# Loading stacked attention operands in fewer, taller pieces, storing their parts earlier, and reordering the router, the output projection and the last layers

## What is computed

```python
x = x + _layernorm(_L0_attn_ref(_layernorm(x), wq, wk, wv, wo))        # 16 heads of 64, causal softmax
x = x + _layernorm(_L0_ffn_ref(_layernorm(x), router_w, ...))          # 8 experts of 256, top 2, capacity 640
x = x + _layernorm(_L1_attn_ref(_layernorm(x), qkv, wo))               # 16 heads of 8, rotary, causal softmax
x = x + _layernorm(_L1_ffn_ref(_layernorm(x), fast_b, w_fc, w_proj, u, v, gate))
# _L1_attn_ref, last line:  out.transpose(0, 2, 1, 3).reshape(B, S, D) @ wo.T
# _L1_ffn_ref:  h = bitlinear(x, w_fc) + gate * (x @ v.T @ fast_b.T @ u.T);  r = max(h, 0);  bitlinear(r * r, w_proj)
```

## Time and profile before

| | us |
|---|---|
| three runs | 1238.11, 1240.81, 1241.08; median 1240.81 |
| the profiled execution | 1239.13 |
| its span from first to last instruction | 1237.3 |
| PE busy | 1121.1 (91%) |
| DVE busy | 862.2 (70%) |
| ACT busy | 815.4 (66%) |
| POOL busy | 349.4 (28%) |
| first attention | up to about 545 |
| output projection, norms, router, second biases | 545 to 613 |
| experts | 613 to 738 |
| second attention | 748 to 1174 |
| output projection, norms, last feed-forward | 1174 to 1237 |

### The profile page before, as it was taken

How to read it: one execution, slowest core, us unless ns; L and a number is a source line. 1 busy time by engine, 2 the same in 40 slices (tenths; PEclk the granted TensorE clock), 3 DMA queues, 4 the chain that set the end, 5 groups by cost and what they waited for, 6 DMA issues and landing times.

```text
span 1237.3 us, 28186 instructions
## 1 busy us (share of the span) xinstructions
PE 1121.1 (91%) x10202; PEld 851.2 (69%) x10202; DVE 862.2 (70%) x2486; ACT 815.4 (66%) x1915; POOL 349.4 (28%) x345
## 2 busy tenths in 40 slices
PE   5999999999999999999899976987888888888886
PEld 3787878787888787888576653665566556556674
DVE  6656566565656565645334547999999899999863
ACT  3766666767666666631233434998889889989932
POOL 1974646455464646213001202000000000000043
PEclk8999999999999999999599995998999899999998
DMA  6222223222322323211011043020310202110001
GB/s 161 59 69 76 69 58 77 63 59 64 80 54 70 76 59 75 65 36 34 15 35 43 25 97 46 2 40 27 66 31 10 40 6 36 26 15 2 2 1 34
DMA packets 33627, 58.90 MB, mean 48 GB/s; under 512 B 4906, under 2 KB 18114, under 8 KB 33490
## 3 DMA queue, kind: packets, MB, share of 16 engines
q1 hardware_dynamic: 32690, 55.52, 19.9%
q10 hardware_dynamic: 800, 1.57, 0.4%
HBM read 27.59 MB, written 4.33 MB: 26 GB/s over the span
## 4 chain that ended last, share of the span: by engine, by line
PE 56%; DVE 18%; issue 11%; ACT 7%; POOL 5%; DMA 2%; SPq 1%; ACTq 0%; POOLq 0%; DVEq 0%
PE pT L1278 12%; PE pO L1201 12%; PE pS L1239 10%; DVE Zb L956 9%; PE pS L1352 4%; ACT probs L719 3%; PE pT L1149 3%; PE pT L1365 3%; DVE Sm L971 3%; PE pS L1313 2%; PE pT L1153 2%; PE pS L1430 1%; ACT PT L699 1%; PE pS L1410 1%; DMA KS<-split 1%
## 5 line engine op out<-in xcount | busy, mean ns | idle before, releaser
L1278 PE MATMUL pT<-cst,probs 128*128 128x128 f32 x2304 | 369.9, 287 | 53.4 <-ACT probs L719 49.2
L1278 PEld LDWEIGHTS pT<-cst,probs 128*128 128x128 f32 x2304 | 257.0, 143 | 149.0 <-ACT probs L719 99.7
L719 ACT ACTIVATE probs<-probs,nmax 128x128 f32<-128x128 f32 (+7 forms) x256 | 198.7, 776 | 129.9 <-DVE nmax L966 128.9
L699 ACT COPY PT<-pT 128x512 f32<-128x512 f32 (+3 forms) x576 | 263.9, 482 | 16.8 <-PE pT L1278 15.6
L966 DVE CUSTOM_DVE_ANT_0 probs<-pS,causal_wide 128x128 f32<-128x128 f32 (+7 forms) x256 | 192.0, 750 | 91.2 <-PE pS L1239 83.6
L719 ACT ACTIVATE probs<-Sm,nmax 128x128 f32<-128x128 f32 (+7 forms) x256 | 199.6, 780 | 55.4 <-DVE nmax L971 49.1
L1201 PE MATMUL pO<-PT,V 128*64 128x128 f32 (+1 forms) x4608 | 233.5, 281 | 2.5 <-DVE attnT L925 1.1
L956 DVE TENSOR_SCALAR Zb<-pS 128x128 bf16<-128x128 f32 (+7 forms) x256 | 192.7, 753 | 20.0 <-PE pS L1245 19.4
L1201 PEld LDWEIGHTS pO<-PT,V 128*64 128x64 f32 (+1 forms) x4608 | 180.9, 114 | 36.3 <-issue 21.0
L971 DVE CUSTOM_DVE_ANT_0 Sm<-pS,Zb 128x128 f32<-128x128 f32 (+7 forms) x256 | 193.3, 755 | 4.5
L543 POOL TENSOR_TENSOR rstd<-rstd,power 128x4 f32<-128x4 f32 x32 | 32.6, 1019 | 552.4 <-DVE rstd L824 552.4
(11 more groups left out here) (189 smaller groups left out, 1370.2 us busy)
## 6 DMA issues: line engine op xcount, KB each, us to landing
wq_t<-factors SPq DMA_DIRECT2D x32, 256.0 KB, 4.0
Qs<-Ql SPq DMA_DIRECT2D x30, 256.0 KB, 3.7
Kh<-Kh SPq DMA_DIRECT2D x30, 256.0 KB, 3.4
Kl<-Kl SPq DMA_DIRECT2D x30, 256.0 KB, 4.6
QS<-split SPq DMA_DIRECT2D x72, 64.0 KB
KS<-split SPq DMA_DIRECT2D x72, 64.0 KB
w1s<-in_w SPq DMA_DIRECT2D x16, 128.0 KB, 2.3
w2s<-in_w SPq DMA_DIRECT2D x16, 128.0 KB, 2.2
```

The source lines that it names most:

```text
L699: nc.scalar.copy(PT[:, g % 2, h, k0 * P:(k0 + nk) * P], pT[r % TBANKS][:, 0:nk * P])\
L719: nc.scalar.activation(probs[:, i % NPROB, 0:n], src[:, 0:n], ACT.Exp, bias=nmax[:, i % 4:i % 4 + 1], scale=-1.0, accum_out=total).then_in ...
L1278: m = nc.tensor.transpose(pT[r % TBANKS][:, kt * P:(kt + 1) * P], probs[:, item % NPROB, (k0 + kt) * P:(k0 + kt + 1) * P], ident)
```

## The change

- **Stacks.** The DRAM tensor is laid out by heads, and the query parts are written three times, once for each key part they are paired with (`split_q`), so that the 72 rows of QS lie behind one another. `stacks` issues 2 loads for QS (64 and 8 rows) and 3 for KS (24 rows each). The bytes loaded are the same.
- **Stores.** One part at a time: 3 DMAs for a query part and 1 for a key part, 12 for a batch (3.1 MB, before 1.6 MB). Those of the first batch move from ACT's queue to SP's, around the loads of the last expert's weights: part 0 of both ahead of w1 of m = 15, the others between w1 and w2.
- **Output projection of the second attention.** SP gathers the 16 heads' rows of `attn1T` into a tile `compact` (4 copies of 8 rows by 4 KB for each half, 32 in all, issued behind the loads of the stacks), and one product for each tile replaces four.
- **Router.** The preparation of `w1e`, `w2e` and `lowA` moves behind `up(0)` on PE and behind `gelus(0)` on ACT; the logits of bank j - 1 are computed right after the transposes of bank j. A wait for the copies of `w1e` and `w2e` stands before the third bank of the gate weights' transposes.
- **Last feed-forward.** The first products of bank j come ahead of the second product of bank j - 1. The normed input goes to `xn3`, another place.

```diff
-        split = nc.dram_tensor("split", (2, PARTS, D, T), BF16, kind="Internal").ap()
+        split_q = nc.dram_tensor("split_q", (HEADS, PARTS, PARTS, DH1, T), BF16, kind="Internal").ap()
+        split_k = nc.dram_tensor("split_k", (HEADS, PARTS, DH1, T), BF16, kind="Internal").ap()
...
+            def store(i, parts):
+                cols = slice(i // 2 * S, (i // 2 + 1) * S)
+                for k in parts:
+                    if k < 2:
+                        sp.wait_ge(part_a, split_step_of(i, k))
+                    else:
+                        sp.wait_ge(part_v, split_step_of(i, 1))
+                    for to in [split_q[:, k, j, :, cols] for j in range(PARTS)] if i % 2 == 0 else [split_k[:, k, :, cols]]:
+                        sp.dma_start(to, part_of(i)[:, k, :]).then_inc(part_stored, 16)
+
             for m in range(2, B * E):
                 e = m % E
+                if m == B * E - 1:
+                    store(0, (0,))
+                    store(1, (0,))
                 sp.wait_ge(up_done, (m - 1) * per_batch)
                 sp.dma_start(w1s[:, m % 2, :], w1[e, :, :]).then_inc(ld_w1[m % 2], 16)
+                if m == B * E - 1:
+                    store(0, (1, 2))
+                    store(1, (1, 2))
                 sp.wait_ge(down_done, (m - 1) * (S // BANK))
...
+                q_rows = split_q[heads, :, :, :, cols].rearrange("h i j d s -> (i j d) h s")
+                k_rows = split_k[heads, :, :, cols].rearrange("h j d s -> (j d) h s")
+                for lo, hi in ((0, 64), (64, STACK)):
+                    sp.dma_start(QS[lo:hi, half % 2, :, :], q_rows[lo:hi, :, :]).then_inc(ld_stack[half % 2], 16)
                 for i in range(PARTS):
...
+                    sp.dma_start(KS[i * (PARTS * DH1):(i + 1) * (PARTS * DH1), half % 2, :, :], k_rows).then_inc(ld_stack[half % 2], 16)
...
+            def gather(half):
...
+                sp.wait_ge(A[1]["n"], (half + 1) * ST)
+                for h in range(HPG):
+                    row = (g * HPG + h) * DH1
+                    sp.dma_start(compact[row:row + DH1, b, :], attn1T[h * (P // HPG):h * (P // HPG) + DH1, b, g, :])\
+                        .then_inc(ld_compact[b], 16)
+
             for half in range(2, G1 * B):
                 sp.wait_ge(A[1]["s"], (half - 1) * (L[1].per // B))
                 if half == G1:
-                    sp.wait_ge(part_stored, 64)
+                    sp.wait_ge(part_stored, 2 * STORED)
                 stacks(half)
                 if half == 2:
-                    store(2)
-                    store(3)
+                    store(2, range(PARTS))
+                    store(3, range(PARTS))
+                gather(half - 2)
+            gather(G1 * B - 2)
+            gather(G1 * B - 1)
...
                 if i == 3 and j == 0:
-                    act.wait_ge(part_stored, 48)
+                    act.wait_ge(part_stored, STORED + 16 * PARTS * PARTS)
...
-                if m == E + 6:
-                    for i in range(2):
-                        act.wait_ge(part_a, split_step_of(i, 1))
-                        act.wait_ge(part_v, split_step_of(i, 1))
-                        nc.scalar.dma_start(split_of(i), part_of(i)).then_inc(part_stored, 16)
...
             pe.wait_ge(zeros_ready, 3)
-            pe.wait_ge(xnT_ready[1], NB)
-            for n in range(NT):
-                nc.tensor.matmul(bank[4][:, n * E:(n + 1) * E], xnT[:, n * P:(n + 1) * P], rws[:, :],
-                                 start=(n == 0), stop=False, skip_group_check=True)
+            for j in range(NB + 1):
+                if j < NB:
+                    pe.wait_ge(xn_ready[1], j + 1)
+                    for t in range(TPB):
+                        i = nc.tensor.transpose(bank[4 + j][:, t * P:(t + 1) * P], xn[:, j * TPB + t, :], ident)
+                    i.then_inc(tr_done[1], 1)
+                if j >= 1:
+                    pe.wait_ge(xnT_ready[1], j)
+                    for n in range((j - 1) * TPB, j * TPB):
+                        nc.tensor.matmul(bank[4][:, n * E:(n + 1) * E], xnT[:, n * P:(n + 1) * P], rws[:, :],
+                                         start=(n == 0), stop=False, skip_group_check=True)
...
             up(0)
+
+
+            nc.tensor.matmul(bank[7][0:RANK, 0:D], fbs[:, :], vs[:, :], start=True, stop=True).then_inc(lowA_done, 1)
...
+            for f in range(FC1):
+                nc.tensor.matmul(bank[7][:, f * P:(f + 1) * P], lowA[:, :], uTs[:, f * P:(f + 1) * P], start=True, stop=False)
+                m = nc.tensor.matmul(bank[7][:, f * P:(f + 1) * P], wfc[:, f, :], ident, start=False, stop=True)
+            m.then_inc(w1e_done, 1)
             pe.wait_ge(r_, 8 + NT)
...
             for n in range(NT):
+                if n == 2 * TPB:
+                    pe.wait_ge(we_ready, 2)
...
             for n in range(NT):
-                for g in range(G1):
-                    m = nc.tensor.matmul(bank[n // TPB][:, (n % TPB) * P:(n % TPB + 1) * P],
-                                         attn1T[:, n // ST, g, (n % ST) * P:(n % ST + 1) * P], wo1s[:, g, :],
-                                         start=(g == 0), stop=(g == G1 - 1))
+                if n % ST == 0:
+                    pe.wait_ge(ld_compact[n // ST], 16 * HEADS)
+                m = nc.tensor.matmul(bank[n // TPB][:, (n % TPB) * P:(n % TPB + 1) * P],
+                                     compact[:, n // ST, (n % ST) * P:(n % ST + 1) * P], wo1s[:, :], start=True, stop=True)
```

More of the change, by code:

```diff
@@ L748, in _ @@
             attention(0)
-            act.wait_ge(lowA_done, 1)
-            nc.scalar.activation(lowA[:, :], bank[4][0:RANK, 0:D], ACT.Copy, scale=gates[:, 0:1]).then_inc(lowA_ready, 1)
-            act.wait_ge(w1e_done, 1)
-            nc.scalar.copy(w1e[:, :], bank[5]).then_inc(we_ready, 1)
-            act.wait_ge(w2e_done, 1)
-            nc.scalar.copy(w2e[:, :, :], bank[6]).then_inc(we_ready, 1)
             copies_T(1)
@@ L772, in _ @@
             gelus(0)
+            act.wait_ge(lowA_done, 1)
+            nc.scalar.activation(lowA[:, :], bank[7][0:RANK, 0:D], ACT.Copy, scale=gates[:, 0:1]).then_inc(lowA_ready, 1)
+            act.wait_ge(w2e_done, 1)
+            nc.scalar.copy(w2e[:, :, :], bank[6]).then_inc(we_ready, 1)
+            act.wait_ge(w1e_done, 1)
+            nc.scalar.copy(w1e[:, :], bank[7]).then_inc(we_ready, 1)
             for j in range(NB):
```

70 lines of the change are left out of this document (26 added, 44 removed).

## The result

| | before | after |
|---|---|---|
| median of the runs, us | 1239.46 | 1223.05 |
| lowest and highest, us | 1237.72, 1241.08 | 1220.11, 1227.99 |
| the profiled execution, us | 1239.13 | 1220.11 |
| its span, us | 1237.3 | 1218.3 |

The ratio after to before is 0.9872, with an interval of 0.9835 to 0.9909. The forecast was 1221 us.

A forecast was written before the change was run, and what follows sets the result against it. It took serial chains around the attentions as the bound, not PE's average load. Router 2.5, stacks 8.0 and end 8.3 made 18.8 us, giving 1220.3 from the profiled execution or 1222.0 by median; forecast 1221, range 1213 to 1229.

The forecast's parts named there:

- Router, 2.5 forecast: Router: of 3.85 us gained on the logits, 2.5 us kept, as PE's moved preparation becomes the last before the ranks.
- The logits: 3.85 forecast: Router: logits of banks 0 and 1 done earlier in PE's idle time, so up(0) could start 3.85 us earlier.
- The preparation as the new last one: Router: with w1e and w2e prepared behind up(0), PE reaches the ranks at 598.2, DVE being ready at 596.85.
- the clock was at 0.5 for nearly all of 586 to 617: Router stage: reason given for taking 2.5 us there, not the 10 us of a full clock.
- the rival with full clock: Router stage: denser PE work holds the clock at 1.0, giving 10 us instead of 2.5, total 1213.5; chance 0.12.
- Its old place cost nothing: Router: the preparation lay between 574 and 578.3, while DVE still normed banks 2 and 3, so it was free.
- Stores, forecast 10.3 us: First batch's stores around the last weights: 3.14 MB at 381 GB/s, landed at 729.8, 1.2 us later than before.
- Loads, forecast 9.8 us: First stack's loads: 7.5 us, between 5.1 and 11, plus 2.3 us around them; before, 19.0 us.
- The first score, forecast at 739.6: Start of the second attention: first stack there at 739.6 instead of 747.62, 8.0 us gained, between 4.5 and 9.1.
- The weights of m = 15, hidden by 0.5 us: Last expert: w1 lands near 725.5 behind stores, up(15) wants it at 726.0; at most 1.5 us at risk.
- The cast at step 51, hidden by 3.3 us: Second attention: second batch's query stores land by 854.2, 3.3 us before ACT's cast at 857.55 asks for them.
- Projection and last layer, 8.3 forecast: Output projection starts 2.9 us earlier, feed-forward rounds take 8.6 instead of 9.29 us; 8.3 us in all, bounds 5.0 and 10.

The follow-up runs named there:

- the second stack held: The kernel after, with the second stack's loads held back until the first stack has landed; 1222.91 us.
- the stacks alone: The kernel before with only the new split-tensor layout, the stores around the last weights and the tall loads; ratio 0.9956, 5.4 us faster.

## Why the prediction came out as it did

The total was right and its parts were not: router and attention gave 6.7 us more than forecast, stacks and end 6.1 us less. That the sum of the two profiled executions came out at 19.0 against 18.8 is luck. Of the signs named beforehand, the DMA rate over 130 GB/s in the loads, the ranks behind PE's own preparation, the cast that did not wait, y(3) right behind y(2) and the early first statistics held; the first score within 2 us of the clearing (5.7) and up(15) not waiting (0.56) did not.

- **Router, 2.5 forecast, 5.0 between the two traces, 5.4 as a mean over traces.** The logits: 3.85 forecast, 2.92 measured (7.90 us from the last transposes to up(0) before, 4.98 after; over all traces 7.2 to 9.5 with the old router and 4.98 or 4.99 with both edits, 3.5 by the means). I took the transposes at the full clock of the earlier trace rows, 0.45 us, and they and the 16 logits ran at half clock. The preparation as the new last one: its delay was forecast at 1.35 us, and the gate transposes came 0.85 us later behind up(0) than before (11.65 us instead of 10.80). These two make 2.1, by the means over traces 2.9, close to the forecast. The rest is the clock behind the ranks: 3.7 us to up(1) and 0.75 lost again from there to the clearing, with the 0.56 of up(15). My step "the clock was at 0.5 for nearly all of 586 to 617" was a reading of one execution; the rival with full clock was half right. "Its old place cost nothing" was true of the kernel before and not of the interleaved one, a question that the sum never asked.
- **Stores, forecast 10.3 us, 13.1.** The step that failed is 381 GB/s, one window of 2 us. Over 10 us it was 307 at full DMA engines. In seven traces the stores took 12.4 to 14.1 us.
- **Loads, forecast 9.8 us with what lies around them, 12.3.** With the second stack held they took 10.1: the price of the pieces of 64 and 24 rows was right to 0.3 us, between bounds of 5 and 11. What was missing is the second stack, issued right behind the first. Behind the 2.3 us around them that leaves 7.8 us for the bytes; the port estimate quoted from the Trainium skill's "SBUF — State Buffer", "Door 1: The DMA port swizzle", was 7.
- **The first score, forecast at 739.6, came at 739.39.** That looks exact and is not: the forecast is on the clock of before, without the router's gain. Everything ahead had moved 4.7 us forward, and the stall behind the clearing was 5.7 us instead of 1.2. Against the two traces of before the stacks are worth 3.6 us, by the mean stall over traces 5.2, by the timing of the stacks alone 5.4 (about 2.6 to 8.3, from its interval), where 8.0 was forecast.
- **The weights of m = 15, hidden by 0.5 us.** PE waited 0.56 us for them, and this cost nothing, as PE waited for the stack behind them anyway (5.7 us behind the clearing).
- **The cast at step 51, hidden by 3.3 us.** It did not wait. ACT's casts in after are as far apart as in the earlier trace rows or closer:

```profile
838.59 1.03 ACT L693 CAST parts<-rot 128x1024 bf16<-128x1024 f32 x1
847.34 1.03 ACT L693 CAST parts<-rot 128x1024 bf16<-128x1024 f32 x1
```

- **Projection and last layer, 8.3 forecast, 6.6 (6.4 by the means of five traces each).** The start was right (2.7 against 2.9), as were the rounds (8.48 against 8.6) and y(3) right behind y(2). Missed were 1.05 us for the clock, which falls where PE waits for gathers and norms, and 0.4 on the order (4.96 against 5.4). That the last gathers cost nothing was right for the wait and wrong for the clock behind it.
- **Second attention, 0 forecast, 4.2 between the traces.** No part of the change. I had added the sum to the profiled execution's own time, and that execution had a dip in its clock which the profiled one of after lacked. By medians the gain is 16.4 us. The means of the traces give 5.4 for the router, 5.2 for the stacks, 0.5 for the attention and 6.4 for the end, 17.5 together.

By the Trainium skill, "TensorE: Matmul & The Clock Gate", "Part 1: The HAM clock gate", the same kernel can show a different number of slow instructions from run to run. The kernel before agrees: the two rows of its second biases took 5.49 and 1.91 us in one execution, 2.94 and 1.38 in the other.

## What to carry to other kernels

A transfer that is on the path can be slowed by those issued right behind it (12.3 us against 10.1 here); hold back what is wanted later, and issue stores as early as their parts exist. Two edits on one in-order engine can be worth little alone (2.0 and 0.0 us here, each within its noise of nothing) and 5 us together, so ask of a step "hidden before" whether it is still hidden after the other edit. A clock level read in one execution is a sample: where a stage has idle time of PE in it, put both levels in the range, and compare stages by several traces before a cause is named.

## What the runs showed that I had not expected

The granted clock late in the second attention differs between executions of one kernel (0.95 or 1.00 over 960 to 1060), and with it its length (426.8 or 422.9 us), by a third of a per cent of the whole. Stores of 128 rows of 2 KB from one queue, with w1 and w2 among them, settled at 307 GB/s over 10 us with the DMA engines full, and at 303 with a pitch of 2 KB instead of 4. SP's issue of one store took 0.63 us while the engines were free (1.89 for three at 714.02) and 0.83 when they were full (4.98 for six at 717.25). That full engines slow the issue fits, and is not shown.
